# A selective-scan layer with a feed-forward matrix: steps at a block's edge reordered, and three scalings moved from ScalarE to GpSimd

## What is computed

```
n    = layernorm(x)
xp,z = split(n @ in_proj_w)                  # 1024 -> 2 x 2048 channels
xc   = silu(conv_b + sum_k conv_w[k] * xp shifted by k)      # 4 taps in time
dt_r, B, C = rmsnorm of the 64, 16 and 16 columns of xc @ x_proj_w.T
dt   = softplus(dt_r @ dt_proj_w.T + dt_bias)
h    = exp(dt * A) * h + dt * B * xc         # 16 states per channel, step by step in time
y    = (sum over states of h * C + D * xc) * silu(z)
x    = x + y @ out_proj_w.T
out  = x + layernorm(x) @ W.T + bias         # W = scales * (codes - 128), blocks of 32
```

## Time and profile before

| | us |
|---|---|
| median of 3 runs | 4553.35 |
| profiled execution, its own time | 4553.78 |
| its span in the trace | 4552.0 |
| TensorE busy | 4257.0 (94%) |
| VectorE busy | 4156.6 (91%) |
| GpSimd busy | 3887.0 (85%) |
| ScalarE busy | 3534.8 (78%) |
| steps j = 2 to 4 and 6, from scan 0 to scan 0 (chunk 8) | 32.26 each |
| last step, first step, second step (chunks 8 and 9) | 37.15, 36.25, 33.58 |

### The profile page before, as it was taken

One profiled execution on the slowest core, in us unless ns is written; L12 is line 12 of the kernel. 1 busy time (PEld: TensorE's weight loads), 2 busy tenths in 40 slices (PEclk: granted clock), 3 DMA queues, 4 the chain that ended last, 5 costly groups with the idle time before them and its releaser, 6 DMA issues.

```text
span 4552.0 us, 77871 instructions
## 1 busy us (share of the span) xinstructions
PE 4257.0 (94%) x25632; PEld 3830.9 (84%) x25632; DVE 4156.6 (91%) x5745; ACT 3534.8 (78%) x8848; POOL 3887.0 (85%) x2894
## 2 busy tenths in 40 slices
PE   7688989999999999999999999999999999998879
PEld 6567778888888888888888888988888898897769
DVE  3899999999999999999999999999999999999871
ACT  3788787888888788787888888787888878888750
POOL 0898989989898998989899898998989899899870
PEclk9788999999999999999999999999999999998889
DMA  7545556575756657575575757557575665755452
GB/s 247 160 122 184 150 183 184 164 224 174 220 166 196 192 174 220 163 227 163 176 218 165 234 155 219 175 156 242 155 226 168 209 189 147 226 167 178 133 150 85
DMA packets 201348, 828.91 MB, mean 182 GB/s; under 512 B 25456, under 2 KB 34416, under 8 KB 151792
## 3 DMA queue, kind: packets, MB, share of 16 engines
q1 hardware_dynamic: 141296, 639.35, 38.6%
q0 software_dynamic: 41216, 151.01, 18.7%
q10 hardware_dynamic: 18432, 33.56, 2.0%
HBM read 634.57 MB, written 55.05 MB: 151 GB/s over the span
## 4 chain that ended last, share of the span: by engine, by line
PE 60%; POOL 19%; DVE 10%; issue 7%; ACT 2%; DMA 1%; SPq 0%; POOLq 0%; DVEq 0%; ACTq 0%
PE ys L646 14%; POOL dbx L494 12%; PE gx L626 12%; PE ys L606 12%; PE g L799 10%; PE g L721 7%; DVE hb L1416 6%; POOL half L518 3%; POOL half L512 3%; DVE gx L1298 1%; PE ys L636 1%; PE hb L901 1%; DVE hc L1364 1%; DMA ybuf<-in_wf_scales 1%; POOL hd L507 1%
## 5 line engine op out<-in xcount | busy, mean ns | idle before, releaser
L494 POOL TENSOR_TENSOR dbx<-dtx,bb 128x1024 f32<-128x1024 f32 x1024 | 2427.4, 2370 | 231.1 <-DVE hb L1416 183.8
L1416 DVE TENSOR_TENSOR_SCAN hb<-hb,dbx 128x512 f32<-128x512 f32 x2048 | 2495.6, 1219 | 55.4 <-ACT hb L1111 27.3
L1111 ACT ACTIVATE hb<-dt,a_neg 128x256 f32<-128x256 f32 x4096 | 1789.1, 468 | 66.3
L606 PE MATMUL ys<-half,ident 128*128 128x256 f32 x3072 | 811.6, 400 | 162.6 <-POOL half L512 93.6
L799 PEld LDWEIGHTS g<-wo,ybuf 128*128 128x128 f32 x7680 | 919.2, 194 | 30.7 <-issue 14.7
L646 PE MATMUL ys<-xnT,wz 128*128 128x256 f32 x4096 | 926.2, 385 | 11.4 <-DVE ybuf L1375 11.4
L799 PE MATMUL g<-wo,ybuf 128*128 128x128 f32 x7680 | 928.3, 277 | 8.4 <-issue 8.4
L626 PE MATMUL gx<-xnT,wx 128*128 128x256 f32 x3968 | 895.4, 383 | 21.5 <-issue 10.9
L646 PEld LDWEIGHTS ys<-xnT,wz 128*128 128x128 f32 x4096 | 782.6, 193 | 127.8 <-DVE ybuf L1375 22.8
L626 PEld LDWEIGHTS gx<-xnT,wx 128*128 128x128 f32 x3968 | 750.6, 192 | 127.3 <-issue 14.3
L606 PEld LDWEIGHTS ys<-half,ident 128*128 128x128 f32 x3072 | 567.4, 195 | 302.2 <-POOL half L512 125.0
(11 more groups left out here) (108 smaller groups left out, 3145.5 us busy)
## 6 DMA issues: line engine op xcount, KB each, us to landing
wz<-in_win SPq DMA_DIRECT2D x128, 1024.0 KB, 5.0
hd<-hd POOLq DMA_DIRECT2D x256, 512.0 KB, 6.3
wx<-in_win SPq DMA_DIRECT2D x124, 1024.0 KB, 5.0
wo<-in_wout SPq DMA_DIRECT2D x123, 1024.0 KB, 7.3
wf<-wf_scratch SPq DMA_DIRECT2D x113, 512.0 KB, 3.6
xc_scratch<-xcn ACTq DMA_DIRECT2D x128, 256.0 KB, 2.7
xcs<-xc_scratch SPq DMA_DIRECT2D x128, 256.0 KB, 5.2
bb<-bc_scratch SPq DMA_DIRECT2D x64, 512.0 KB, 9.6
```

What stands on the lines that cost most here:

```text
L494: nc.gpsimd.tensor_tensor(dbx[:, k % 2, :].rearrange("p (n t) -> p n t", n=NQ), dtx[:, S % 2, a, :].unsqueeze(1).to_broadcast([P, NQ, T]), ...
L606: mm = nc.tensor.matmul(ys[i // 3][:, 0:T], ident[:], half[:, n % PLACES, w * T:(w + 1) * T], start=False, stop=(i % 3 == 2 and w == 1), s ...
L1111: ins = nc.scalar.activation(h[:, m * T:(m + 1) * T], dt[:, j % 2, a, :], ACT.Exp, scale=a_neg[:, ds((2 * j + a) * N + 2 * v + m, 1)])
L1416: nc.vector.tensor_tensor_scan(h[:], h[:], dbx[:, k % 2, w * UW:(w + 1) * UW], 0.0, ALU.mult, ALU.add).then_inc(scans, 1)
```

## The change

In the last step the order of TensorE, of ScalarE and VectorE around the taps, and of SyncE's loads is another one; the second norm's first rows are made at the end of the last step instead of in the first, a step sooner, and the second rows after unit 1 of the first; the first gate of an edge step comes a product later; GpSimd does the six scalings in two instructions. `out_proj(lo, hi)` now takes tiles of 16 rather than a part of 4. rms_ready counts two per chunk. Waits and index changes that follow from this are left out here.

```diff
@@ SyncE
                     if last and st.inproj:
                         bc_rows(c + 1)
-                        for q in range(2):
-                            load_b(c + 1, q)
-                            load_c(c + 1, q)
-                    if nx.x_job(nx_last):
+                        load_b(c + 1, 0)
+                        load_b(c + 1, 1)
+                        load_c(c + 1, 0)
+                        load_b(c + 1, 2)
+                        load_c(c + 1, 1)
+                        load_b(c + 1, 3)
+                    if not last and nx.x_job(nx_last):
                         load_pair(S + PAIRS + 2)
...
                     if last and st.inproj:
-                        for q in range(2, NQ):
-                            load_b(c + 1, q)
-                            load_c(c + 1, q)
+                        load_c(c + 1, 2)
+                    if last and nx.x_job(nx_last):
+                        load_pair(S + PAIRS + 2)
+                    if last and st.inproj:
+                        load_c(c + 1, 3)
@@ GpSimd
+            def chunk_scale(chunk):
+                pool.wait_ge(rms_r, after(chunk + 1))
+                pool.wait_ge(ss_tr, after(chunk))
+                nc.gpsimd.tensor_tensor(
+                    ssn[:, :, BC:EO].rearrange("p t (g n) -> p t g n", g=2),
+                    ssm[:, :, R:E].rearrange("p t (g n) -> p t g n", g=2),
+                    ssq[:, 2:6].rearrange("p (t g) -> p t g", t=TT).unsqueeze(3).to_broadcast([P, TT, 2, N]),
+                    ALU.mult).then_inc(rms_ready, 1)
+                nc.gpsimd.tensor_tensor(ssn[:, :, 0:R], ssm[:, :, 0:R],
+                                        ssq[:, 0:2].unsqueeze(2).to_broadcast([P, TT, R]), ALU.mult
+                                        ).then_inc(rms_ready, 1)
...
                     products(5)
+                    if last and st.inproj:
+                        chunk_scale(c + 1)
                     group_sum(S, 0, 1)
@@ TensorE, the last step
                         norm1(0)
                         x_proj()
-                        out_proj(0)
+                        out_proj(0, 4)
                         norm1(1)
-                        out_proj(1)
+                        out_proj(4, 8)
                         norm1(2)
-                        out_proj(2)
+                        out_proj(8, 10)
                         norm1(3)
+                        out_proj(10, 12)
                         x_in_proj(0)
                         ss_transpose()
-                        out_proj(3)
+                        x_in_proj(1)
                         dt_proj()
-                        x_in_proj(1)
                         group(0)
                         group(1)
                         group(2)
+                        out_proj(12, 16)
@@ TensorE, the first step
-                        out_proj(0)
-                        out_proj(1)
+                        norm2(0)
+                        out_proj(0, 4)
+                        norm2(1)
+                        out_proj(4, 8)
+                        norm2(2)
                         x_proj()
-                        out_proj(2)
-                        norm2(0)
-                        out_proj(3)
-                        norm2(1)
+                        norm2(3)
+                        out_proj(8, 12)
+                        x_in_proj(0)
                         group(0)
                         dt_proj()
-                        norm2(2)
+                        x_in_proj(1)
                         group(1)
-                        norm2(3)
-                        x_in_proj(0)
                         group(2)
-                        x_in_proj(1)
+                        out_proj(12, 16)
@@ ScalarE
                 nc.scalar.activation(ssq[:], ssq[:], ACT.Exp, scale=-0.5).then_inc(rms_r, 1)
-                act.wait_ge(rms_r, after(chunk + 1))
-                act.wait_ge(ss_tr, after(chunk))
-                for tt in range(TT):
-                    nc.scalar.activation(ssn[:, tt, 0:R], ssm[:, tt, 0:R], ACT.Identity,
-                                         scale=ssq[:, tt:tt + 1])
...
                     unit(1)
+                    norm2_second_row()
                     unit(2)
-                    norm2_start()
...
-                    norm2_row(0)
...
-                    norm2_row(1)
...
                     unit(12)
-                    if not edge:
+                    if not edge or last:
                         x_taps()
                     dt_softplus()
                     unit(13)
                     first_decays_out()
                     second_skip_term()
                     unit(14)
-                    if edge:
+                    if edge and not last:
                         x_taps()
                     unit(15)
+                    norm2_first_row()
@@ VectorE
                     product(11)
-                    y_gate(S, 0)
                     if not edge:
+                        y_gate(S, 0)
+                    if not edge or last:
                         taps()
                     scan(13)
                     product(12)
-                    add_out()
-                    norm_stats()
+                    if edge:
+                        y_gate(S, 0)
+                    else:
+                        add_out()
+                        norm_stats()
                     scan(14)
                     product(13)
                     if edge:
+                        add_out()
+                        norm_stats()
+                    if edge and not last:
                         taps()
```

More of the change, by code:

```diff
@@ L660, in chunk_ss @@
             def chunk_ss(chunk):
-                pe.wait_ge(rms_ready, after(chunk + 1))
+                pe.wait_ge(rms_ready, after(2 * (chunk + 1)))
                 for tt in range(TT):
@@ L782, in z_in_proj, with out_proj @@
                         pair_z(S + 1, a)
[L784 removed]
+                    def out_proj(lo, hi):
                         if not st.outproj:
                             return
[L787 removed]
+                        if lo == 0:
                             pe.wait_ge(wo_in, landed(PAIRS // 2 + S - PAIRS + 1))
@@ L794, in out_proj @@
                                 g1_after_o()
-                        for kt in range(part * TILES // 4, (part + 1) * TILES // 4):
+                        for kt in range(lo, hi):
                             for tt in range(TT):
@@ L803, in out_proj @@
                                                       stop=(kt == TILES - 1), skip_group_check=True)
-                        if part == 3:
+                        if hi == TILES:
                             mm.then_inc(o_mm, 1)
@@ L1016, in chunk_rms @@
                 act.wait_ge(rms_ln, after(chunk + 1))
+                act.wait_ge(rms_ready, after(2 * chunk))
                 nc.scalar.activation(ssq[:], ssq[:], ACT.Exp, scale=-0.5).then_inc(rms_r, 1)
-                act.wait_ge(rms_r, after(chunk + 1))
-                act.wait_ge(ss_tr, after(chunk))
-                for tt in range(TT):
-                    nc.scalar.activation(ssn[:, tt, 0:R], ssm[:, tt, 0:R], ACT.Identity,
-                                         scale=ssq[:, tt:tt + 1])
[L1024 to L1028, removed]
             def chunk_ss_out(chunk):
@@ L1168, in norm1, with norm2_first_row, norm2_second_row @@
                             norm_evac(xnT[:, st.parity], 4 * (c + 2), i, gx, l1_tr, l1_evac)
-                    def norm2_start():
-                        if first and st.ffn:
-                            norm2_begin(c - 2)
-                    def norm2_row(tt):
-                        if first and st.ffn:
-                            act.wait_ge(l1_tr, after(4 * min(c + 2, NC)))
-                            norm2_rows(c - 2, tt)
+                    def norm2_first_row():
+                        if last and st.outproj:
+                            norm2_begin(c - 1)
+                            act.wait_ge(l1_tr, after(4 * min(c + 3, NC)))
+                            norm2_rows(c - 1, 0)
+                    def norm2_second_row():
+                        if first and st.ffn:
+                            norm2_rows(c - 2, 1)
                     def norm1_start():
@@ L1250, in _ @@
             LAST = NC * PAIRS
-            norm2_begin(NC - 2)
-            act.wait_ge(l1_tr, after(4 * NC))
-            act.wait_ge(l2_tr, after(4 * (NC - 2)))
-            for tt in range(TT):
-                norm2_rows(NC - 2, tt)
+            norm2_rows(NC - 2, 1)
             act.wait_ge(f_mm, after(LAST - 2 * PAIRS))
@@ L1307, in pair_ss @@
                 if q % PAIRS == 0:
-                    dve.wait_ge(rms_ready, after(q // PAIRS))
+                    dve.wait_ge(rms_ready, after(2 * (q // PAIRS)))
                     nc.vector.tensor_scalar(ssm[:], src, 1.0, None, ALU.mult).then_inc(xp_add, 1)
```

17 lines of the change are left out of this document (9 added, 8 removed).

## The result

The changed kernel takes 4607.83 us (median of 4 runs, 4606.54 to 4611.0) where the kernel before takes 4553.97 (4 runs beside it): ratio 1.012 [1.0108, 1.0132], so it is **54 us slower**. The prediction was 4537, faster, with a range up to 4560. Its sign was wrong and the time lies outside the range. The profiled execution took 4606.54, its span is 4604.7.

The account below looks back on a forecast made before the run. VectorE and TensorE were taken as full in regular steps, with the loss at 13 chunk edges; 1.3 us an edge gives 17 us off 4553.78, so 4537 us, range 4513 to 4560.

Parts of the forecast that it names:

- Other parts: B's rows, SyncE's load queue, prologue scaling and tail: no gain, and loads in time.
- All covered, the first by 2 us: SyncE's weight and row loads land before they are due; output weights at 2546.1, wanted at 2548.
- The new wait: Last step: unit 13 behind taps and softplus; VectorE idles 2 us before scan 13, TensorE 3.1 before z.
- 2.4 us later: Last step: TensorE waits 3.1 us for the gate and starts z at 2533.85, 2.4 us later than before.
- the edge that was taken for all: The profiled last, first and second steps, 37.15, 36.25 and 33.58 us, stood for all 13 edges, gaining 1.3 each.
- Forecast 105.6 for the three steps: Step lengths after the change: last about 37.4, first 34.4, second 33.8 us.
- rival (c): GpSimd's scaling is dear: slower from 2.05 us; at 3.5 an edge loses 1.45, total 4573; chance 0.15.
- the line drawn in the prediction: GpSimd's two scalings: linear at 2.1 ns per element between two measured rows, 0.33 + 0.47, taken as 0.75 us.
- Nothing gained: B's rows ahead of the weights end GpSimd's 1.85 us wait, but GpSimd has slack there.
- (a): Lateness of z doesn't arise, unit 13 not held by the taps: edge gains 3.0 us, total 4515; chance 0.16.
- (b): The chain eats the gain, 1 us more in the first step or x_proj wait: no change, 4550; chance 0.21.

Follow-up runs that it names:

- e5: Changed kernel with the bias DMA issued between the first step's two accumulating sums, right behind the first: 4554.2 us, 1.0009 of the kernel before.
- e9: e5 with the last two output tiles held until ScalarE's first decays of the next step, splitting TensorE's idle time before z: 4547.38 us, 0.9984.
- e3: Changed kernel with SyncE's order of B, C and weight loads at the last step as before the change: 4611.66 us, 1.013.
- e4: Kernel before with only GpSimd's scaling of dt, B and C, in two instructions after products(5), instead of ScalarE's: 4544.06 us, 0.9982.
- e7: e5 with the last step's taps as before the change, behind unit 14 and scan 14: 4512.48 us, 0.9918.
- e11: e7 with ScalarE making unit 13 ahead of softplus in the last step: 4504.25 us, 0.9892.
- e2: Changed kernel with the first step's bias DMA issued earlier, after products(3), ahead of the first sum and not the second: 4593.78 us, 1.0093.
- e8: Changed kernel with both weight loads of the first step held until the second sum landed, bias still right ahead of it: 4559.1 us, one run.
- e10: Changed kernel with only the last step's taps as before, bias still ahead of the second sum: 4588.0 us, 1.0076.

## Why the prediction was wrong, step by step

**The step that failed** is the end of "Other parts": "All covered, the first by 2 us". It listed SyncE's loads with issue, landing and due time, and left out GpSimd's own DMAs. The second adding sum of the first step was due 11.8 us after its issue before (2567.09 to 2578.92) and is due 9.6 after it now (2595.80 to 2610.67 less the wait of 5.26). With the old landing of 8.9 that would do, with 14.8 it is 5.2 us late. The margin was thin in any case: over the 13 edges the old landings went up to 12.6, and five of them were over 9.6. The prediction also said only that the x weights go out "near 2536" in the last step and asked whether *they* are in time; in the first step they go out 3.8 us behind the sum before and 2.7 ahead of it after, and the question was whom they delay. Price, from the table: 38.35 against 33.88 in e5, which differs in nothing but the bias's place, 4.5 us an edge, **58 us**. The runs put it on two neighbours together: with the bias 3.1 us ahead of the sum, it lands in 13.7 to 15.2 with both weight loads beside it, 11.4 to 13.2 with one, and 7.1 to 9.0 with none (one run); with both loads and the bias 14.8 ahead, in up to 11.0. Removing either neighbour is enough for the wait.

Not all of the 58 is waiting. In three second steps of the change the granted clock stayed at 1.00, as in chunk 10's:

```profile
2875.78:2912.52 36.74, 34.07 (x209) 30.66 (x208) 32.20 (x45) 26.10 (x65) 30.42 (x23) 1.00 0.62 181
```

There GpSimd waits 4.2 to 4.3 for the sum and the step is 2.8 to 2.9 longer than in e5: a wait costs its length less some 1.4. The waits of all 13 edges are 64.6 us, which less 13 x 1.4 makes 46. The other 12 are, by this estimate, the low clock again: behind TensorE's 2.2 to 3.6 us of idle time for the halved tile it fell in ten of the 13 second steps (0.91 to 0.96 on their mean).

**The second miss** is in "The new wait". Its time was right: VectorE waits 1.90 for scan 13 (2 forecast), TensorE idles 3.28 (3.1 forecast). Its price was taken as z being "2.4 us later"; that z would then itself run slower was nowhere. z ends another 1.7 us later, up to 2.9, in most chunks. In e5 the mean first step is 35.12 where 34.43 is the undisturbed one: 0.7 us an edge, 9 us. e9 gives 7 of them back.

The rest of e5's 17 us above the forecast is small things: the edge that was taken for all, 37.15 + 36.25 + 33.58 = 106.98, is 0.23 above the mean of 106.75 (3 us); the undisturbed steps of e5 are 105.84 for 105.6 (3 us); and outside the 13 edges e5 is 3 us longer than before where the forecast had nothing (4 more in chunk 14's last step and chunk 15, 1 less at the start).

**Sum, after the fact.** Forecast 105.6 for the three steps, after 110.76: 13 x 5.16 = 67 us of the 70 between 4537 and 4607. Of these 58 are the late sum with the clock behind it, 6 the first step (34.89 for 34.4) with the clock behind z's wait, 3 the rest.

**What was right.** These readings of after answer to the earlier trace rows. The two scalings on GpSimd:

```profile
2547.90 0.30 POOL L539 TENSOR_TENSOR ssn<-ssm,ssq 128x64 f32<-128x64 f32 x1
2548.15 0.40 POOL L544 TENSOR_TENSOR ssn<-ssm,ssq 128x128 f32<-128x128 f32 x1
```

0.65 together for 0.75 forecast, so rival (c) is out; the four-dimensional pattern and the broadcast scalars cost nothing that shows beside the line drawn in the prediction (0.33 and 0.47). And VectorE's waits over the edge, each where and about as long as forecast:

```profile
2558.85 1.23 DVE L1430 TENSOR_TENSOR_SCAN hb<-hb,dbx 128x512 f32<-128x512 f32 x1 [1.90 <-ACT hb L1128]
...
2568.17 1.23 DVE L1430 TENSOR_TENSOR_SCAN hb<-hb,dbx 128x512 f32<-128x512 f32 x1 [1.82 <-ACT hb L1128]
...
2582.22 0.36 DVE L1324 TENSOR_SCALAR ssm<-ys 128x192 f32<-128x192 f32 x1 [0.54 <-PE ys L659]
```

Scan 13 waits 1.90, scan 0 of the first step 1.82 (1.9 forecast), the x projection's result 0.54 (1 forecast). Scan 9 no longer waits.

Softplus with its two table loads takes 3.27 again (2554.48 to 2557.75) and has no room for the drain that the Trainium skill (ScalarE: Activation LUTs, What ACT_TABLE_LOAD costs) puts beside each load: scan 13's wait would be 2.8 us longer by it and is 1.90.

"Nothing gained" for B's rows was about right in the changed kernel, by e3 (4 us, no more than two sets differ by). But GpSimd had no slack for that wait in the kernel before: e4 shows 8 us from B's rows a microsecond sooner.

**The rivals.** (a) said z need not be late, with unit 13 not held by the taps, at 4515. That is e7, 4512.48, and e11 goes further. The mechanism was right, but it is not what this change does. (b) and (c) did not come about. None of the rivals had a transfer of GpSimd's in it; the one that had to end on the slower side looked for the price of an instruction and not for a landing.

**What stays open.** Why a sum directly behind the bias is the one delayed, in e2 the first, in the change the second: the runs show it, not how GpSimd's queue and the DMA engines share their work. That the bias ahead of it alone delays it little rests on one run, e8, in which z's weights are held back too. Why the clock stays up in some chunks after the same 3.28 us of idle time. In e10, whether the sum is later because the loads come closer or because of the rows beside it. Whether the bias between the sums would also help the kernel before was not tried.

## What to carry to other kernels

When an order is rewritten, list every transfer of the stretch with issue, landing and due time, those that the compute engines issue themselves too, and ask of each load that moves up whom it slows, not only whether it is in time itself. An unbroken idle time of TensorE ahead of a long block of matmuls may cost more than its length; before it is accepted, look in the trace for the granted clock behind it. If a new wait appears behind a long instruction on another engine, first look for a short unit there that needs none of it: moving unit 13 was worth some 10 us (13 x 0.75 by the step lengths).

## What was not expected of the hardware

The adding DMA of `hd` (512 f32 elements a partition) has no duration of its own: 4.5 to 18.1 us from issue to landing in these runs, and moving the bias or the loads near it moved it. The longest in each kernel with the bias 3.1 us ahead and two weight loads beside it were 15.2, 16.1 (e3) and 18.1 (e10), and the same bias in another place of the same queue took up to 17.1 with no harm. TensorE's granted clock fell to 0.50 for some 3.4 us, in two edges twice that, around z after 3.28 us of idle time, in 11 of 13 edges of the change; after 2.43 in 12 of 13 of e9; and after 2.2 to 3.6 in 10 of the 13 second steps of the change. z never ran at the low clock in the kernels that idled 1 us or less ahead of it (before, e4, e7, e10, e11).
